# Head groups of four and single key chunks in two attentions, and copies moved from VectorE to ScalarE

## The reference, cut to what matters

```python
x = x + L0_xattn(layernorm(x), ctx)           # 1601 keys, dense softmax
x = x + L0_ffn(layernorm(x))                  # 9 experts, top 2, hidden 352
x = x + L1_xattn(layernorm(x), ctx, itok)     # each query picks 64 of 256 keys, with repeats
x = x + L1_ffn(layernorm(x))                  # 8 experts, top 2, and a shared one, hidden 176
# L0_xattn
attn = softmax(einsum('bhnd,bhmd->bhnm', q * 8**-0.5, k)); out = einsum('bhnm,bhmd->bhnd', attn, v) @ Wo + bo
# L1_xattn: c_kv = x_kv @ W_kv_down.T; c_sel = c_kv[b, indices]; kv = c_sel @ W_kv_up.T; softmax over the 64 picked
```

## Time and profile before

| | |
|---|---|
| Time, median of 3 runs | 1535.59 us (1530.25 to 1536.47) |
| The profiled execution: time, span | 1533.95 us, 1531.8 us |
| PE busy | 1395.9 us, 91% |
| DVE busy | 1092.1 us, 71% |
| ACT busy | 789.7 us, 52% |
| POOL busy | 828.1 us, 54% |
| Mean granted clock of PE | 0.964 of full speed |

### The profile page before, as it was taken

The page is one execution under the profiler, slowest core; times in us unless marked ns, Lnnn a source line. Parts: engine busy times, 40 slices in busy tenths (PEclk is TensorE's granted clock), DMA queues, the critical chain, the costliest instruction groups (busy, mean ns, idle before and its releaser), DMA issues.

```text
span 1531.8 us, 34069 instructions
## 1 busy us (share of the span) xinstructions
PE 1395.9 (91%) x12588; PEld 804.0 (52%) x12588; DVE 1092.1 (71%) x2283; ACT 789.7 (52%) x1200; POOL 828.1 (54%) x1381
## 2 busy tenths in 40 slices
PE   4899799999999999999999999999999999997987
PEld 2244464357533674347743575346843477334845
DVE  4885578866787668877688667876588776865663
ACT  3457337652575426772376524764266723773451
POOL 4356346755566545664457544675456644544462
PEclk8799899999998999999999999999999999997997
DMA  4505310132102330023201421023300331000111
GB/s 111 144 22 150 81 48 12 30 100 66 34 19 49 90 82 2 22 78 86 55 2 34 96 74 36 12 67 79 83 2 23 77 89 26 1 7 28 41 41 45
DMA packets 97654, 82.12 MB, mean 54 GB/s; under 512 B 17658, under 2 KB 90644, under 8 KB 97492
## 3 DMA queue, kind: packets, MB, share of 16 engines
q1 hardware_dynamic: 96916, 78.72, 19.8%
q10 hardware_dynamic: 576, 1.23, 0.3%
HBM read 67.29 MB, written 12.61 MB: 52 GB/s over the span
## 4 chain that ended last, share of the span: by engine, by line
PE 63%; DVE 20%; ACT 5%; POOL 5%; issue 4%; DMA 1%; SPq 0%; ACTq 0%; POOLq 0%; DVEq 0%
PE ob L788 10%; PE um L846 8%; PE ob L863 7%; DVE mx L1259 7%; PE um L847 7%; PE um L773 6%; PE um L758 6%; PE um L736 4%; ACT probs L1054 2%; DVE mx L1376 2%; DVE big L1372 2%; DVE xn L1157 2%; PE um L830 2%; PE um L913 2%; PE um L730 1%
## 5 line engine op out<-in xcount | busy, mean ns | idle before, releaser
L1259 DVE TENSOR_REDUCE mx<-um 128x2 f32<-128x802 f32 (+1 forms) x512 | 501.6, 989 | 177.3 <-PE um L758 173.6
L1054 ACT ACTIVATE probs<-um 128x1024 f32<-128x1024 f32 (+1 forms) x448 | 425.7, 963 | 215.2 <-PE um L773 211.0
L1452 POOL TENSOR_TENSOR hid<-hid,cwb 128x256 f32<-128x256 f32 (+1 forms) x304 | 217.0, 732 | 265.3 <-DVE hid L1271 130.2
L1060 ACT ACTIVATE hid<-um 128x256 f32<-128x256 f32 (+1 forms) x304 | 116.7, 384 | 346.0 <-PE um L847 336.8
L1458 POOL TENSOR_TENSOR big<-iotab,idx_lo 128x512 bf16<-128x512 bf16 x256 | 272.0, 1078 | 28.3 <-PE um L953 20.4
L788 PE MATMUL ob<-probs,vaug 128*9 128x256 f32 (+1 forms) x3328 | 280.6, 386 | 3.2 <-ACT oT L1035 2.7
L758 PE MATMUL um<-kst,qa 64*128 64x401 bf16 (+1 forms) x1024 | 178.4, 347 | 25.3 <-DMA kst<-k_parts 9.8
L773 PE MATMUL um<-big,kst 64*128 64x256 bf16 (+1 forms) x1664 | 171.1, 280 | 14.5 <-DVE mx L1376 4.8
L1271 DVE TENSOR_TENSOR hid<-hid,um 128x256 f32<-128x256 f32 (+1 forms) x304 | 124.4, 414 | 55.8 <-ACT hid L1060 53.0
L846 PE MATMUL um<-xnT,w1T 128*128 128x256 f32 (+1 forms) x400 | 129.3, 406 | 0.0
L863 PE MATMUL ob<-w2T,hid 128*128 128x128 f32 (+1 forms) x800 | 124.2, 280 | 4.6 <-POOL hid L1452 3.7
(11 more groups left out here) (221 smaller groups left out, 2087.9 us busy)
## 6 DMA issues: line engine op xcount, KB each, us to landing
kst<-k_parts SPq DMA_DIRECT2D x360, 50.0 KB
cwb<-cw_rows SPq DMA_DIRECT2D x112, 128.0 KB, 3.4
k_parts<-big SPq DMA_DIRECT2D x72, 128.0 KB, 1.9
ctx_sb<-in_ctx SPq DMA_DIRECT2D x7, 768.0 KB
cwb<-cw_rows SPq DMA_DIRECT2D x48, 96.0 KB, 3.0
k1st<-k_parts SPq DMA_DIRECT2D x96, 32.0 KB
cwb<-cw_rows SPq DMA_DIRECT2D x48, 64.0 KB, 2.7
cwb<-cw_rows SPq DMA_DIRECT2D x16, 112.0 KB, 3.0
```

The costliest lines, as they stand in the source:

```text
L1054: act.activation(probs[0:kn, k:k + 2, 0:w], own_banks, ACT.Exp).then_inc(f_read, 1)
L1060: act.activation(hid[0:nr, own % NHID, :], quarter[place[ev][0]][0:nr, 0:NQ], ACT.Silu).then_inc(th_ready, 1)
L1259: dve.tensor_reduce(mx[:, p % 2, s, :, j], pair[:, :, 0:w], AX, ALU.max, negate=True).then_inc(u_read, 1)
L1452: pool.tensor_tensor(h, h, cwb[0:nr, k, :], ALU.mult).then_inc(hw_ready, 1)
```

## The change

1. Layer 0: `s0` and `w0` take four heads and one chunk of keys, instead of two heads and two chunks. 52 groups in a batch (4 times 13) instead of 56. The four strips of PE are now the four heads, and `ob` holds four heads' sums. `q0`, `ev0` and `c0` come 4 times in a batch instead of 8; `comb` has 36 columns instead of 18.
2. Layer 1: `s1` and `mu` take four heads and one of the two chunks (8 each, as before); `w1` is 8 matmuls that add up over both chunks, 4 times in a batch instead of 8; so are `q1` and `c1`. `qp1` has one slot of four heads instead of two of a pair, and `probs1` holds one group.
3. ACT instead of DVE copies `cnt`, `q1`, `c0` and `c1`, in all batches. `q0` stays on DVE, 512 columns wide.
4. New numbers in `AT` and `SHIFT`. The 52 groups are spread over the same 56 units (`GU` = 56/52). The second half of the `part`s of a batch stands closer together ('pxs' 0.8 instead of 1.201), and in batch 0 there are 20 `part`s ahead of the first `q0` instead of 12 ('first' 16 instead of 8).

```diff
-AT = {..., 'first': 8, ..., 'pxs': 1.201, ..., 'le0': 7.981, 'rt0': 8.969, ...}
+AT = {..., 'first': 16, ..., 'pxs': 0.8, ..., 'le0': 7.019, 'rt0': 8.007, ..., 's1c': 0.5}
...
-        comb = sb("comb", [P, 2 * V1])
+        comb = sb("comb", [P, 4 * V1])
...
-        NG = (KC + 1) // 2
-        NGB = NP * NG
+        NG = KC
+        NGB = NF * NG
...
+        GU = XL / NGB
...
-                return own + t - t % 1.0 + AT["psn"]
+                return own + GU * (t - t % 1.0) + AT["psn"]
...
+                for k in range(NF):
+                    t = first + step * (2 * k + 1)
+                    for c in range(KC1):
+                        put(t + AT["s1"] + AT["s1c"] * step * c, "s1", b, KC1 * k + c)
+                        put(t + AT["mu"] + AT["s1c"] * step * c, "mu", b, KC1 * k + c)
+                    put(t + AT["q1"], "q1", b, k)
+                    put(t + AT["w1"] + AT["s1c"] * step, "w1", b, k)
+                    put(t + AT["c1"] + AT["s1c"] * step, "c1", b, k)
...
             def scores(b, g):
-                for c in chunks(j):
-                    kn = rows(c, NK)
+                for a in range(2):
                     for hh in range(2):
                         o = SLOT * hh
-                        m = pe.matmul(own[hh][0:kn, (c % 2) * NQ:(c % 2 + 1) * NQ], kst[o:o + SLOT, p, c * P:c * P + kn],
-                                      qp[o:o + SLOT, p % 2, :], start=True, stop=True)
+                        m = pe.matmul(own[hh][0:kn, a * NQ:(a + 1) * NQ], kst[o:o + SLOT, 2 * k + a, c * P:c * P + kn],
+                                      qp[o:o + SLOT, k % 2, a, :], start=True, stop=True)
...
             def weigh(b, g):
-                        q = QD * (2 * hh + c % 2)
+                        q = QD * (2 * a + hh)
-                                      start=(j == 0), stop=(c + 2 >= KC), skip_group_check=True, tile_position=(0, q))
+                                      start=(c == 0), stop=(c == KC - 1), skip_group_check=True, tile_position=(0, q))
...
+            def weigh1(b, k):
+                bank = free_bank(("w1", b, k))
                 for c in range(KC1):
+                    pe.wait_ge(mulp, NP * b + KC1 * k + c + 1)
+                    for a in range(2):
+                        for hh in range(2):
...
             # ACT
+                elif kind == "q1":
+                    if NF * b + n >= 1:
+                        act.wait_ge(f_psum, fill["s1", b - (n == 0), (KC1 * n - 1) % NP] + 1)
+                    copy(qp1[:, :, :].rearrange("p a q -> p (a q)"), bank.bitcast(bf16)[:, 0:2 * NQ]).then_inc(f_read, 1)
+                elif kind in ("c0", "c1"):
...
+                elif kind == "cnt":
...
                 elif kind == "s1":
                     if n >= 2:
-                        act.wait_ge(f_psum, fill["w1", b, n - 2] + 1)
+                        act.wait_ge(f_psum, fill["w1", b, n // KC1 - 1] + 1)
```

196 lines of the change are left out of this document (85 added, 111 removed).

## The result

The changed kernel is slower: 1559.07 us (median of 4 runs, 1553.48 to 1565.03) against 1536.03 us for the kernel before beside it (1530.25 to 1540.23), ratio 1.0157, 95% interval 1.0114 to 1.0199. The forecast was 1498 us, range 1471 to 1523. The profiled execution took 1556.69 us, its span 1554.9.

A forecast was written before the change was run, and what follows sets the result against it. TensorE, 94% busy from 190 to 1330 us, was taken to set the pace. 1533.95 - 57.8 (its savings) + 14 (attention waits) + 4 (start) + 2 (end) = 1496.2 us, 1498 at the median's level; range 1471 to 1523.

The forecast's parts named there:

- I take 2 us for each of the seven attentions 1 to 7, 14 in all: Loss from TensorE and VectorE waiting for each other in attentions, set against the saving: 14 us.
- The 38.5 us: Work estimated for VectorE and for TensorE alike between groups 8 and 28 of an attention in the new order.
- R1: Rival: VectorE and ScalarE pace most of the attention, half or more of the saving goes; 1519 us, chance 0.22.
- The upper bound: Most that waits in an attention could take back: its whole saving, 7.2 us.
- Near 105 us instead of 110.6: Sign of success: length of a layer 0 attention from its first to its last group.
- unchanged. Nothing.: TensorE's `part`, `pair1`, `s1` and FFN work: no time gained or lost.
- (a) to (d): TensorE savings: combinations 34.5, half-filled `w0` groups 17.3, half-filled `s0` groups 5, `keep_clock` 1; together 57.8 us.
- VectorE's relief: Copies leaving VectorE and fewer `q0` copies: 9.0 us less work per batch, by itself no time gained.
- The start: Batch 0, first `q0` behind 20 `part`s instead of 12: first `s0` 7.4 us later, 4 us lost.
- The end: Last batch's layer 1 attention, standing alone: 2 us lost, between 4 gained and 6 lost.
- The copies on ScalarE: In attentions, 3.8 us more ScalarE work per batch, hidden by TensorE: costed at nothing.
- R3: Rival: slower, gaps in the attentions grow until TensorE's clock falls; 1567 us, chance 0.07.

The follow-up runs named there:

- e5: Kernel after with each maximum reduction reading only the first half of its columns (result differs): 1502.9 us, ratio 0.9784 to the kernel before.
- e6: Kernel before with each maximum reduction reading only the first half of its columns (result differs): 1517.3 us, ratio 0.9879.
- e9: Kernel before with copies on ScalarE and only the second attention in groups of four heads: 1565.7 us, ratio 1.0189 to the kernel before.
- e14: Kernel before with the spacing of its reductions ('pxs') at 1.1 instead of 1.201: 1554.5 us, ratio 1.0141.
- e18: Kernel before with the spacing of its reductions ('pxs') widened from 1.201 to 1.25: 1568.0 us, ratio 1.0264.
- e15: Kernel before with the second attention's multiplications 0.8 of a group later and its weighted sums 0.4 later: 1617.5 us, ratio 1.0541.
- e8: Kernel after with the order's numbers of before, other than three that the groups need, and no single shifts: 1550.2 us, ratio 1.0118 to before.
- e10: Kernel after with fourteen numbers of before put back (router, mask, norms' steps, key loads): 1573.6 us, ratio 1.0246 to before.
- e11: Kernel after with the `pair1` reduction of the second attention's pairs 4 and 6 some 0.8 of a group earlier: 1566.1 us, ratio 1.0188 to before.
- e12: Kernel after with the second attention's multiplications 0.8 of a group later and its weighted sums 0.4 later: 1610.1 us, ratio 1.0496 to before.
- e16: Kernel after with one more idle 512-column matmul ahead of the scores of groups 28 to 41 in every batch: 1576.9 us, ratio 1.0288 to before.
- e2: Kernel before with `cnt`, `q1`, `c0` and `c1` copied by ScalarE instead of VectorE: 1539.4 us, ratio 1.0039.
- e3: Kernel after with the copies of `cnt`, `q1`, `c0` and `c1` back on VectorE: 1567.1 us, ratio 1.0239 to the kernel before.
- e1: Kernel before with the second half of each batch's `part` reductions denser ('pxs' 0.86 instead of 1.201): 1599.6 us, ratio 1.0422.

## Why the prediction was wrong, point by point

- **The step that failed** is "I take 2 us for each of the seven attentions 1 to 7, 14 in all". Measured: attentions 1 to 6 are 0.8 us longer and attention 7 is 1.8 longer, so against the 7.2 forecast each they give back some 53 us. The idle time at full clock rose from 8.7 to 14.0 us an attention. The kind of loss was right, its size was not. e5 and e6 show what sets it: 14 us off VectorE's reductions are worth 4.9 us in after and 0.8 in before. The 38.5 us that the prediction found for VectorE and TensorE alike in groups 8 to 28 was the sign: in the first half of an attention the two are busy 48.6 and 47.6 of 55.9 us, neither without gaps. R1 was the right reading of it; R1's 5 us an attention was still too little; it left the second attention's chain out, which e9 shows. The test named for R1, more than 50 us of TensorE's waits for the reductions and exponentials, was met: 56.8 us between 190 and 1330 us after, where the same kinds of waits were 14.1 before,

```profile
PE um L778 <- DVE mx L1265: 16.8, 25, 1.3
...
PE um L763 <- DVE mx L1265: 12.2, 18, 1.2
PE um L778 <- DVE mx L1366: 11.9, 6, 2.1
PE ob L868 <- POOL hid L1442: 11.0, 6, 3.9
PE um L778 <- ACT probs L1058: 10.5, 18, 1.2
PE um L763 <- DVE mx L1366: 5.4, 18, 0.3
```

without its fourth row, which lies behind the attentions.
- **The upper bound was wrong too.** It was put at the whole 7.2 us of an attention, and the range was added up with 35 us for seven, 5 each, where that bound makes 50. A new order is not bounded by what it saves: e14, e18 and e15 lose 3, 6 and 13 us an attention without a change of work (six attentions 653, 670 and 715 for 635).
- **The yardstick was a slow attention.** "Near 105 us instead of 110.6" took the longest of before, with a clock of 0.94; before, the six have a mean of 105.9. After, it is 106.0, which that sign would have taken for a success.
- **"unchanged. Nothing."** for the stretches behind the attentions failed: 19.3 us (4.3 + 15.0). Of the 15.0, 8.2 are rest (19.8 for 11.6) and 6.8 are longer busy time (434.7 for 427.9): before, the clock was 1.00 in all six stretches; after, it was 0.98 in three of them, where TensorE was busy some 1.5 us more than in the other three. After, TensorE waited for POOL's expert rows (L868) 11.0 us in 6 times between 190 and 1330 us; before it was 0.4. e8 took back 10 us of the 15 and e10 none, so which of the numbers does it stays open.
- **(a) to (d)**: by form and count right. By time, attention 0 fell by 6.8 us. It has no second attention beside it, so no `c1`, but all of `keep_clock`: its part of (a) to (d) is 2.2 + 2.2 + 0.6 + 1 = 6.0 us, not 7.2, and eight `part`s of 2.1 us have left it. In the full attentions at full clock TensorE's busy time fell by 5.3, though its groups of combinations and last chunks fell by 7.8 (8.9 to 4.4, 4.3 to 1.9 and 2.4 to 1.5): probably because an operation beside a gap counts with its whole 0.62 us, one in a full queue with 0.56. The total is 1371, not 1340.
- **VectorE's relief** was put at 9.0 us a batch, 72 in all; its busy time fell by 48.4. Some 70 us of copies went, but among others `eq` took 84.5 us for 73.7 and the norms' `xn` 41.5 for 33.4, the same operations in another place of the order.
- **The start**: the first `s0` came at 59.4 where 56 was forecast, 9.9 us later than before for 7.4. Executions differ here: e11, e12 and e16, with after's start, have it at 67.3, 59.4 and 62.0, and e14, e15 and e18, with before's, at 52.1, 51.3 and 48.7. Of the 2.1 us of `part`s that moved ahead, attention 0 gave back 0.8 at most (6.8 less 6.0); so some 9 us instead of 4.
- **The end**: 1.9 us gained behind attention 7 where 2 lost were forecast; the other way, but inside its bounds of 4 gained to 6 lost.
- **The copies on ScalarE** at nothing: e2 says +0.4% (1.0007 to 1.0070); e3's interval overlaps that of after. Nearly right. After shows the 512-column bf16 copy at 0.596 us on ScalarE and 0.418 on VectorE, so a factor of 1.4. The ratio of ScalarE: Activation LUTs, Rules for kernel authors, in the Trainium skill, up to about 3 in bf16, would by the prediction's estimate have made them 26 us of work.
- **The rivals**: R3 named the end that came (slower, 1567), its chance was 0.07. Its point of decision, 7.2 us an attention in waits and clock, was reached almost exactly (7.3); its clock was not: 0.98 between 190 and 1330 us, above the 0.97 that was named for it. In the attentions the waits did it at the clock of before; only in the stretches behind them did the clock have a part, some 5 us. So R3 came near the time, but not by its spells inside the attentions. In the experiments the clock does more: e1, e15 and e18 have 26, 29 and 16 us more rest in six attentions than before, and 37, 51 and 19 us more busy time of the same matmuls. TensorE: Matmul & The Clock Gate, HAM oscillation, in the Trainium skill speaks of waits that throttle a kernel again and again; these three runs agree, with 0.90 to 0.96 for before's 0.98, and e14, with 16 us more rest and 0.99, does not.

## What to carry to other kernels

In this kernel, work taken off the busiest engine was worth its time only where the second engine did not get denser. So add up both engines' work in the densest stretch, and where the two sums are equal, give the whole saving back in one rival with a large chance. The sum is a sign and not a measure, as e3 shows: how long the reductions took mattered, and 25 us more of other work for VectorE did not. Where an order was tuned number by number, a change of structure starts from an untuned one, and its loss is not bounded by the work that it moves; price that as a rival with a large chance, not as a rest. And test such a theory by making the suspected engine's work lighter in both kernels, which changes the load and leaves the order; moving things tests load and order at once. Take the yardstick from several stretches, not from one.
